# Comparing the second half of each edge list with three destinations, in a graph network kernel

## What is computed

```python
edge_index = jnp.stack([src, dst])
agg = jax.ops.segment_sum(edge_attr, dst, num_segments=N)      # edge features, per destination
h_sum = jax.ops.segment_sum(h[src], dst, num_segments=N)       # in several layers
deg = jax.ops.segment_sum(ones, dst, num_segments=N)
```

## Time and profile before

| what | us |
|---|---|
| median of 3 executions | 850.17 |
| lowest and highest | 847.88 and 850.56 |
| span of the profiled execution | 857.5 |
| of it the counting stage, up to the end of the last L1629 | 256.8 |

### The profile page before, as it was taken

How to read it: one execution, slowest core, us unless ns; L and a number is a source line. 1 busy time by engine, 2 the same in 40 slices (tenths; PEclk the granted TensorE clock), 3 DMA queues, 4 the chain that set the end, 5 groups by cost and what they waited for, 6 DMA issues and landing times.

```text
span 857.5 us, 16017 instructions
## 1 busy us (share of the span) xinstructions
PE 789.4 (92%) x6335; PEld 713.4 (83%) x6335; DVE 610.7 (71%) x973; ACT 325.1 (38%) x580; POOL 21.8 (3%) x39
## 2 busy tenths in 40 slices
PE   5699999998997999989998999969987999999995
PEld 2589999998997999889998998535546999699994
DVE  6998999998886676777876874657567455035654
ACT  0234545454356322332245332345335332432233
POOL 3500000000000000000000000000000000000000
PEclk9558999999797999999998999989999999999998
DMA  5446787877662100000000000000000000000001
GB/s 106 100 102 139 159 188 164 190 167 166 146 132 54 39 1 1 1 2 1 1 1 21 1 1 3 0 1 13 1 0 26 0 0 1 1 1 1 1 25 52
DMA packets 161334, 43.00 MB, mean 50 GB/s; under 512 B 155080, under 2 KB 159761, under 8 KB 161189
## 3 DMA queue, kind: packets, MB, share of 16 engines
q1 hardware_dynamic: 148042, 39.81, 20.8%
q10 hardware_dynamic: 11932, 0.81, 1.0%
q0 software_dynamic: 1280, 1.29, 0.6%
HBM read 39.07 MB, written 2.01 MB: 48 GB/s over the span
## 4 chain that ended last, share of the span: by engine, by line
PE 76%; DVE 12%; SPq 4%; issue 3%; DMA 2%; ACT 2%; POOL 0%; DVEq 0%; ACTq 0%
PE bank L1694 20%; PE bank L1695 20%; PE bank L1629 11%; PE bank L1619 7%; PE bank L1902 2%; SPq L551 2%; PE bank L1910 1%; PE bank L1756 1%; PE bank L1953 1%; PE bank L1954 1%; PE bank L1707 1%; SPq L553 1%; PE bank L1769 1%; DVE wb L1236 1%; DVE counts L968 1%
## 5 line engine op out<-in xcount | busy, mean ns | idle before, releaser
L1694 PE MATMUL bank<-stage,f_hi 125*128 125x392 f32 x1000 | 347.8, 348 | 3.5 <-issue 2.2
L1695 PE MATMUL bank<-stage,f_lo 125*128 125x392 f32 x1000 | 341.6, 342 | 0.0
L1114 DVE CAST stage<-counts 125x2352 fp32r<-125x2352 uint8 x120 | 164.3, 1380 | 80.9 <-PE bank L1695 80.7
L776 ACT ACTIVATE stage<-counts 125x1568 fp32r<-125x1568 uint8 x80 | 108.1, 1351 | 226.8 <-PE bank L1695 224.5
L1694 PEld LDWEIGHTS bank<-stage,f_hi 125*128 125x128 f32 x1000 | 189.2, 189 | 5.1 <-issue 4.0
L1695 PEld LDWEIGHTS bank<-stage,f_lo 125*128 125x128 f32 x1000 | 189.1, 189 | 0.6
L1629 PE MATMUL bank<-tmp,wb 128*65 128x25 f32 x2000 | 139.3, 225 | 1.7 <-DVE tmp L1072 1.7
L1629 PEld LDWEIGHTS bank<-tmp,wb 128*65 128x65 f32 x2000 | 136.0, 150 | 2.6 <-DVE tmp L1072 2.4
L729 ACT ACTIVATE counts<-bank 125x500 uint8<-125x500 f32 x188 | 88.6, 537 | 47.3 <-PE bank L1619 45.6
L1619 PE MATMUL bank<-rowb,xT 128*128 128x125 bf16 x1250 | 92.5, 233 | 9.7 <-DVE rowb L1050 5.3
L1047 DVE TENSOR_TENSOR xT<-xT,tmp 128x2560 bf16<-128x2560 bf16 (+1 forms) x63 | 92.8, 1473 | 5.1 <-PE bank L1619 5.0
(11 more groups left out here) (223 smaller groups left out, 670.5 us busy)
## 6 DMA issues: line engine op xcount, KB each, us to landing
wb<-in_edge_attr SPq DMA_DIRECT2D x125, 256.0 KB, 3.9
wa<-in_x SPq DMA_DIRECT2D x12, 125.0 KB
out<-wl SPq DMA_DIRECT2D x6, 250.0 KB
xT<-in_dst SPq DMA_DIRECT2D x63, 4.0 KB, 3.5
xT<-in_dst ACTq DMA_DIRECT2D x62, 4.0 KB, 3.1
eaT<-eaT SPq DMA_DIRECT2D x1, 784.0 KB, 6.3
wb<-in_L_gnn_w_ih SPq DMA_DIRECT2D x1, 384.0 KB, 3.4
gate_w_d<-wl SPq DMA_DIRECT2D x1, 384.0 KB, 3.0
```

The lines of the kernel that those rows point to most:

```text
L776: nc.scalar.activation(set_buffer(u, m), counts[:, SETS[u][0]:sum(SETS[u]), chunk(c)], ACT.Copy).then_inc(s["set_a_ready"], 1)
L1114: nc.vector.tensor_copy(set_buffer(u, m), counts[:, SETS[u][0]:sum(SETS[u]), chunk(pair * 2 + off)]).then_inc(s["set_d_ready"], 1)
L1694: mm(bank[h][:, 0:CH], f_hi[:, first + k, :], rhs[:, k, :], start=(first + k == 0), stop=False)
L1695: last = mm(bank[h][:, 0:CH], f_lo[:, first + k, :], rhs[:, k, :], start=False, stop=(first + k == HI - 1))
```

## The change

Blocks are still 5 destinations with two lists of 128 edges. But the second list is now compared with the destinations 2, 3 and 4 of its block only. So the second matmul of a block has 75 moving columns (L1670 of the new kernel; the first, L1666, keeps 125).

To make these one-hot rows in one VectorE instruction per group, the kept key list becomes eight copies for every two blocks, `PARTS_KEY`: the first list with five shifts (keys minus 0, 25, 50, 75, 100) and the second with three (minus 50, 75, 100). Each copy is compared with 0 to 24. The key comparison writes 128x2000 instead of 128x2500. The two neighbouring elements of the inner dimension are now two blocks, where they were the two lists of a block. The copies are written by ScalarE when lists are kept: eight or sixteen small activations with a constant added instead of one. They lie in three tiles (rowb, wl1, wl3).

The low-digit comparison writes 125 columns per list instead of 128 (128x2500 instead of 128x2560); the columns 125 to 127 are set to zero once by GpSimd, and the weights keep 128 columns.

Lists are now kept 126 blocks at a time, at the blocks 0, 126, 252, 378 and 500, so that a pair of blocks isn't cut. For the last group, whose last block's list is moved back to end at the last edge, the destinations 0 and 1 of the second list are compared too (`oh_last`, one more matmul of 50 columns per block, five in all). A block whose edge in slot 128 still belongs to destination 0 or 1 sets the flag to the general path: two more small VectorE instructions in group 5. GpSimd makes six short iotas where there were two, three memsets and one select more.

```diff
 UNITS = [(g, i, n) for g in range(NGP) for i, n in ((0, 4), (4, 3), (7, 3)) if g * GB + i + n <= NBK] + [(NGP - 1, 4, 1)]
 NU = len(UNITS)
 UB = 5
-QL = 125
-NQ = NBK // QL
+QL = 126
+NQ = 5
+Q_AT = (0, QL, 2 * QL, 3 * QL, NBK + 1 - QL)
 SLOTS = 256
+PARTS_KEY = ((0, 0), (0, 1), (0, 2), (0, 3), (0, 4), (1, 2), (1, 3), (1, 4))
+NK = len(PARTS_KEY)
+KEPT_AT = (0, 270, 540, NBK + 1)
 EW = 25
 NE = N // EW
 TE = 8
...
-        nl, nk = GB * 128 * 2, GB * BK * 2
+        nl, nk = GB * 128 * 2, GB * NK * HI
         oh_lo = [xT_bf[:, r * nl:(r + 1) * nl].rearrange("p (b l j) -> p b l j", l=128, j=2) for r in range(2)]
-        oh_key = [rowb_bf[:, r * nk:(r + 1) * nk].rearrange("p (b k j) -> p b k j", k=BK, j=2) for r in range(2)]
-        key_list = rowb_bf[:, 2 * nk:2 * nk + 2 * NBK].rearrange("p (b j) -> p b j", j=2)
+        oh_key = [rowb_bf[:, r * nk:(r + 1) * nk].rearrange("p (b m k j) -> p b m k j", m=NK, k=HI, j=2) for r in range(2)]
+        nk_list = (KEPT_AT[1] - KEPT_AT[0]) * NK
+        key_list = [a[:, 0:(KEPT_AT[i + 1] - KEPT_AT[i]) * NK].rearrange("p (b m j) -> p b m j", m=NK, j=2)
+                    for i, a in enumerate((rowb_bf[:, 2 * nk:], wl1[:, 400:400 + nk_list // 2].bitcast(BF16), wl3[:, 256:600].bitcast(BF16)))]
+        last_at = NGP * GB - GB
+        key_last = wl3[:, 600:606].bitcast(BF16).rearrange("p (b m j) -> p b m j", m=2, j=2)
         nh = 2 * TE * EW
         oh_dst = [tmp_f[:, r * nh:(r + 1) * nh].rearrange("p (j w) -> p j w", w=EW) for r in range(2)]
-        lo_list = tmp_f[:, 2 * nh:2 * nh + NBK].bitcast(BF16).rearrange("p (b j) -> p b j", j=2)
+        lo_list = tmp_f[:, 2 * nh:2 * nh + NBK + 1].bitcast(BF16).rearrange("p (b j) -> p b j", j=2)
         at = [nl]
 
         def carve(n):
...
         past_block = carve(NQ)
+        past_two = carve(NQ)
+        oh_last = carve(3 * 2 * HI).bitcast(BF16).rearrange("p (b m k j) -> p b m k j", m=2, k=HI, j=2)
         crowded = carve(NQ)
         list_idx = carve(NQ).bitcast(I32)
...
                            allow_small_or_imprecise_dtypes=True)
-            nc.gpsimd.iota(key_base, pattern=[[-QL * BK, NQ]], base=0, channel_multiplier=-BK,
-                           allow_small_or_imprecise_dtypes=True)
-            nc.gpsimd.iota(past_block, pattern=[[QL * BW, NQ]], base=BW, channel_multiplier=BW,
-                           allow_small_or_imprecise_dtypes=True)
+            for a, n in ((0, NQ - 1), (NQ - 1, 1)):
+                nc.gpsimd.iota(key_base[:, a:a + n], pattern=[[-QL * BK, n]], base=-Q_AT[a] * BK, channel_multiplier=-BK,
+                               allow_small_or_imprecise_dtypes=True)
+                nc.gpsimd.iota(past_block[:, a:a + n], pattern=[[QL * BW, n]], base=Q_AT[a] * BW + BW, channel_multiplier=BW,
+                               allow_small_or_imprecise_dtypes=True)
+                nc.gpsimd.iota(past_two[:, a:a + n], pattern=[[QL * BW, n]], base=Q_AT[a] * BW + 2, channel_multiplier=BW,
+                               allow_small_or_imprecise_dtypes=True).then_inc(s["pool_w"], 1)
+            for r in range(2):
+                nc.gpsimd.memset(oh_lo[r][:, :, LO:D, :], 0.0)
+            pool.wait_ge(s["pool_w"], 5)
+            nc.gpsimd.affine_select(out=past_two[:, NQ - 1:NQ], in_=past_two[:, NQ - 1:NQ], compare_op=ALU.is_gt, fill=-1.0, base=last_at - Q_AT[NQ - 1],
+                                    pattern=[[0, 1]], channel_multiplier=-1)
             for r in range(RE):
                 last = nc.gpsimd.memset(ea_in[r][:, :, DE:DE + 1], 1.0)
             last.then_inc(s["slots_clean"], 1)
...
             def keep_lists(q):
 
-                for k, kept in enumerate((lo_list, key_list)):
-                    act.wait_ge(s["list_t"], 2 * q + 2)
-                    nc.scalar.activation(kept[:, q * QL:(q + 1) * QL, :],
-                                         bank[7][:, :].bitcast(BF16)[:, k * 256:(k + 1) * 256].rearrange("p (j c) -> p c j", j=2)[:, 0:QL, :],
-                                         ACT.Copy).then_inc(s["list_kept"], 1)
+                a, b = Q_AT[q], Q_AT[q] + QL
+                turned = [bank[7][:, :].bitcast(BF16)[:, k * 256:(k + 1) * 256].rearrange("p (j c) -> p j c", j=2) for k in range(2)]
+                act.wait_ge(s["list_t"], 2 * q + 2)
+                nc.scalar.activation(lo_list[:, a:b, :], turned[0].rearrange("p j c -> p c j")[:, 0:QL, :], ACT.Copy).then_inc(s["list_kept"], 1)
+                for i, kept in enumerate(key_list):
+                    c, d = max(a, KEPT_AT[i]), min(b, KEPT_AT[i + 1])
+                    if c < d:
+                        for m, (j, w) in enumerate(PARTS_KEY):
+                            last = nc.scalar.activation(kept[:, (c - KEPT_AT[i]) // 2:(d - KEPT_AT[i]) // 2, m, :],
+                                                        turned[1][:, j, c - a:d - a].rearrange("p (b j) -> p b j", j=2), ACT.Copy, bias=-float(HI * w))
+                if q == NQ - 1:
+                    for m in range(2):
+                        last = nc.scalar.activation(key_last[:, :, m, :], turned[1][:, 1, last_at - a:QL].rearrange("p (b j) -> p b j", j=2),
+                                                    ACT.Copy, bias=-float(HI * m))
+                last.then_inc(s["list_kept"], 1)
 
             def odd_list(e):
 
...
-                dve.wait_ge(s["list_kept"], 2 * ((b0 + n - 1) // QL) + 2)
+                dve.wait_ge(s["list_kept"], 2 * min((b0 + n - 1) // QL, NQ - 1) + 2)
                 if g >= 2:
                     dve.wait_ge(s["unit_made"], units_until(g - 2))
-                nc.vector.tensor_tensor(oh_lo[r][:, 0:n, :, :], iota_l.rearrange("p (a l) j -> p a l j", a=1).to_broadcast([128, n, 128, 2]),
-                                        lo_list[:, b0:b0 + n, :].rearrange("p b (a j) -> p b a j", a=1).to_broadcast([128, n, 128, 2]),
+                nc.vector.tensor_tensor(oh_lo[r][:, 0:n, 0:LO, :], iota_l.rearrange("p (a l) j -> p a l j", a=1)[:, :, 0:LO, :].to_broadcast([128, n, LO, 2]),
+                                        lo_list[:, b0:b0 + n, :].rearrange("p b (a j) -> p b a j", a=1).to_broadcast([128, n, LO, 2]),
                                         ALU.is_equal).then_inc(s["lo_hot"], 1)
-                nc.vector.tensor_tensor(oh_key[r][:, 0:n, :, :], iota_l.rearrange("p (a l) j -> p a l j", a=1)[:, :, 0:BK, :].to_broadcast([128, n, BK, 2]),
-                                        key_list[:, b0:b0 + n, :].rearrange("p b (a j) -> p b a j", a=1).to_broadcast([128, n, BK, 2]),
-                                        ALU.is_equal).then_inc(s["key_hot"], 1)
+                half = -(-n // 2)
+                i = sum(b0 >= a for a in KEPT_AT[1:3])
+                here = (b0 - KEPT_AT[i]) // 2
+                hot = nc.vector.tensor_tensor(oh_key[r][:, 0:half, :, :, :].rearrange("p b m k j -> p (b m) k j"),
+                                              iota_l.rearrange("p (a l) j -> p a l j", a=1)[:, :, 0:HI, :].to_broadcast([128, half * NK, HI, 2]),
+                                              key_list[i][:, here:here + half, :, :].rearrange("p b m (a j) -> p (b m) a j", a=1).to_broadcast([128, half * NK, HI, 2]),
+                                              ALU.is_equal)
+                if g == NGP - 1:
+                    hot = nc.vector.tensor_tensor(oh_last.rearrange("p b m k j -> p (b m) k j"),
+                                                  iota_l.rearrange("p (a l) j -> p a l j", a=1)[:, :, 0:HI, :].to_broadcast([128, 6, HI, 2]),
+                                                  key_last.rearrange("p b m (a j) -> p (b m) a j", a=1).to_broadcast([128, 6, HI, 2]),
+                                                  ALU.is_equal)
+                hot.then_inc(s["key_hot"], 1)
                 if 1 <= g + 1 < NQ:
                     make_lists(g + 1)
                 if g == NQ:
...
+                    nc.vector.tensor_tensor(past_two[:QL, :], lists_i.rearrange("p (q s) -> p q s", q=NQ)[:, :, D], past_two[:QL, :],
+                                            ALU.is_lt).then_inc(s["dve_w"], 1)
                     dve.wait_ge(s["dve_w"], landed.next())
-                    nc.vector.tensor_tensor(g_bad[:LO, :], g_bad[:LO, :], g_most[:LO, :], ALU.max).then_inc(s["flag_part"], 1)
+                    nc.vector.tensor_tensor(crowded[:QL, :], crowded[:QL, :], past_two[:QL, :], ALU.max).then_inc(s["dve_w"], 1)
+                    dve.wait_ge(s["dve_w"], landed.next())
+                    nc.vector.tensor_reduce(g_most[:QL, :], crowded[:QL, :], AX.X, ALU.max).then_inc(s["dve_w"], 1)
+                    dve.wait_ge(s["dve_w"], landed.next())
+                    nc.vector.tensor_tensor(g_bad[:QL, :], g_bad[:QL, :], g_most[:QL, :], ALU.max).then_inc(s["flag_part"], 1)
 
                 es = edge_blocks(g)
                 ne = len(es)
...
-                        for j in range(2):
```

(24 more changed lines are left out.)

32 lines of the change are left out of this document (16 added, 16 removed).

## The result

The changed kernel takes 957.16 us (median of four executions, 956.37 to 957.82), against 850.37 us for the kernel before (four executions, 847.88 to 851.75). The ratio is 1.126, with a 95% interval from 1.123 to 1.130. The forecast was 948 us, from 878 to 978.

A forecast was written before the change was run, and what follows sets the result against it. TensorE was taken to bound the kernel at 1.2 GHz (5.56 us a group), with TensorE, VectorE and SyncE close at 2.4. A stage ending 98.3 us later, added to the 850.2 us median, gave 948 us, range 878 to 978.

The forecast's parts named there:

- The clock: Counting stage: the thinner product run no longer suffices to raise TensorE's clock, which stays at 1.2 GHz from about 50 us.
- The faster rival: Counting stage: the clock rises all the same and loads set the pace; 845 us, between 838 and 850; 17%.
- A group at 1.2 GHz: Ten blocks on TensorE in the counting stage: edge sums 3.46 us plus product run 1.68, together 5.14 us.
- The start: Groups 0 to 3: shorter comparisons save 1.2 us, copies cost 0.3; edge sums of group 3 start at 50.8 us.
- The second matmul: TensorE's product matmuls: 75 columns take 63 ns at 1.2 GHz; about 60 ns either way at 2.4, gaining nothing.
- The other bound: Product matmul of 75 columns at 1.2 GHz: 105 ns if something besides moving columns sets it; group stays 5.56 us.
- VectorE: Counting stage comparisons: 540 to 560 fewer elements save 0.3 us, giving 2.97 us a group; key comparison near 1.16 us.
- ScalarE's copies: Keeping lists as small shifted copies: first eight delay the first comparison by nothing to 1.4 us, taken as 0.3.
- The joint behind the stage: Transposes after the counting stage: up to 2.9 us more at 1.2 GHz, hidden behind destination degrees, taken as 0.
- The stage and the span: Counting stage ends at 355.1 us, 98.3 us later; later layers untouched; profiled span 955.8 us.
- the last step: From span to median: the median's distance of 7.3 us below the profiled span is kept, giving 948.5 us.
- SyncE's 3.37 us a group: Issuing a group's loads in the counting stage: 3.37 us, untouched by the change, setting the pace at 2.4 GHz.

The follow-up runs named there:

- b_second_75: Kernel before, second matmul of a block cut to 75 columns in every group, counts wrong; stage ended at 358.4 us, whole execution 23839.9 us with the general path.
- e_before_75_right: Kernel before, second matmul at 75 columns in all groups but the last, which keeps 125, so outputs are right; 961.16 us, ratio 1.130 to the kernel before.
- f_before_100: Kernel before, second matmul at 100 columns in all groups but the last; 970.11 us, ratio 1.141 to the kernel before.
- c_after_edge_50: Changed kernel, each edge-sum matmul moving its 25 columns twice (50); 846.04 us, ratio 0.9944 to the kernel before.
- h_after_edge_50_act: Changed kernel with 50-column edge sums and all destination-number loads issued by ScalarE; 829.82 us, ratio 0.9756 to the kernel before.
- before: The kernel without the change; 850.37 us, median of four executions.
- after: The changed kernel as it was measured, without further edits; 957.16 us, median of four executions.

## Why the prediction was right, and where it was off

The forecast's mechanism is the one that was found, and its range held the time. That the span came out within 1.1 us owes something to luck, since errors of about 2 us cancelled. By its own steps:

- **The clock.** Predicted: once lost about 50 us, it stays at 1.2 GHz to the end of the stage. Measured: 0.50 from 24.1 us on. The kernel before was at 0.50 from 25 us too; what didn't take place is the short rise near 45 us. That cost nothing that can be seen: the edge sums of group 3 start earlier than before all the same. The reason given, that the run of twenty product matmuls sufficed only just, is borne out by the runs: the shorter matmul alone takes the clock away (b_second_75, e_before_75_right), 100 columns don't keep it (f_before_100), and moved columns put back in another line bring it back (c_after_edge_50). It wasn't predicted that edge sums could do as well as the product run. The prediction had said of L1629 only that it never did with its 25 columns.
- **The faster rival**, that a TensorE without pauses comes up all the same, had 17%. The 306.5 us without a pause in e_before_75_right are against it, and c_after_edge_50, less busy and at 2.4 GHz, is too. Part 1 of the Trainium skill's page "TensorE: Matmul & The Clock Gate", which has the clock follow how busy TensorE was, doesn't hold in this trace as it stands: at the same number of matmuls with the same weights, the moving columns made the difference.
- **A group at 1.2 GHz.** Predicted 5.14 us, measured 5.18. The product run is 1.69 us instead of 1.68, L1680 3.49 instead of 3.46. Over 59 groups that is 2.4 us.
- **The start.** The edge sums of group 3, from which the sum counts, were put at 50.8 us, and they start at 48.7. The forecast counted the shorter comparisons (1.2 us) and 0.3 us for the copies. It missed that the kernel before had lost 1.19 us in group 0 waiting for gathered sources, a wait that is gone in this execution, and that the first comparison begins 0.4 us sooner. Why the wait is gone is open. These 2.1 us hide the 2.4 us of the line above.
- **The second matmul.** 63 ns were taken, with 105 as the other bound. A pair now takes 169 ns (1.69 us for ten pairs); with 105 ns for the first, that leaves 64. The other bound is out. At 2.4 GHz the prediction was wrong: it said "about 60 ns either way", so that nothing is gained there. The product run takes 0.96 us instead of 1.18 (h_after_edge_50_act), which is 37 ns for a matmul of 75 columns beside 59 for one of 125. So TensorE, put at 3.04 us a group in the faster rival, isn't what would hold the changed kernel at the full clock; VectorE is, with 2.97. The forecast of 948 us didn't depend on it. The rule of the Trainium skill on LDWEIGHTS ("TensorE: Matmul & The Clock Gate"), 107 ns for 128 weight columns, isn't seen here; its section on weight-path perf modes, by which 128 weights that aren't float32 load faster, agrees.
- **VectorE.** 2.97 us a group predicted, 2.97 measured in c_after_edge_50. L1085 was said to come near 1.16 us; it takes 1.19, and 1.11 to 1.14 us lie between its start and the next one's in c_after_edge_50.
- **ScalarE's copies.** Taken at 0.3 us on the path, measured at 0: the first eight take 1.46 us, some 0.16 us apart, and end at 25.1 us, before the first comparison at 25.6.
- **The joint behind the stage.** L1642's doubling was put at 0, hidden behind the degrees. It is hidden but for its end: the transposes are on the chain of waits, and the flag behind them comes a few tenths of a us later than the degrees would allow.
- **The stage and the span.** Predicted end 355.1 us, measured 355.7. Predicted span 955.8 us, measured 954.7: what follows the stage took 599.0 us, against 600.7 in the profiled execution of before. In the other runs that don't take the general path it is 599.4 to 601.2 us, so most of this is no effect of the change.

**The term that was mis-sized** is the last step, the distance between span and median. "The median of the runs lies 7.3 us below that span, and I keep this distance": that gave 948.5 us instead of 957. The distance was no constant. In after, the profiled execution's time is its span plus 1.7 us, so the profiled execution of before had taken about 859 us, far up among its executions (38 over all comparisons, from 845.19 to 855.86, and one of 860.09). It was one that lost the clock for 13.6 us from 212.8 on the earlier trace rows. If the rest takes some 600 us in every execution, a median one has a stage of about 249 us (an estimate: 850.4 less 1.7 and 600), 8 us less than the profiled 256.8. How the clock went in the others isn't known, as no trace of them was kept, but their mean granted clock falls in the main with the time, from 0.964 at 845.19 us to 0.949 at 855.86, and it was 0.946 in the profiled one. In the changed kernel, where the clock is never up in the stage, there is nothing of the kind to lose: its four executions lie within 1.5 us. The right step was to add the 1.7 us to the new span of 955.8, 957.5 us. Of the two ways to read the change, 97.2 us between spans and 106.8 us between medians, the second is the difference of typical executions.

What the forecast said of the loads, that SyncE's 3.37 us a group would set the pace as soon as VectorE needs less, was priced only in the rival. c_after_edge_50 shows its waits, and h_after_edge_50_act takes them away and gains 16.2 us. What stays open is what decides a short rise in the list groups: b_second_75 had one (39.2 to 42.6 us), and e_before_75_right had none, though the two issue the same instructions up to the last group. So the program alone doesn't decide it, and one profile each doesn't tell more.

## What to carry to other kernels

Before making the matmuls of a tight stage smaller, look at the granted clock of that stage, and at what TensorE moved right before it rose: 40% fewer columns in one of two product matmuls would have saved TensorE 0.2 us a group at 2.4 GHz, where it isn't the bound, and cost 107 us by leaving the engine at 1.2. A thin matmul with few moving columns can be made thicker for next to nothing, as the edge sums were, and this decides for the change or against it (957 or 846 us). And when a shorter comparison should bring a gain, ask which queue is next: here the small loads had to leave SyncE's queue before the 17.5 us could be had.

## What was not expected of the hardware

- TensorE without a pause over 306.5 us and 3073 matmuls stays at 1.2 GHz. With 50 instead of 25 moving columns in the edge sums it holds 2.4 GHz over 194 us with 15 us of pauses. At 2.4 GHz these wider matmuls cost next to nothing: a run of 32 takes 1.90 us in h_after_edge_50_act, and 1.86 us with 25 columns in the kernel before.
- Fewer columns can be faster or slower, depending on the clock. At 1.2 GHz 100 columns give 970 us, 75 give 961, and 125, which bring the clock back, 850.
- At 2.4 GHz a matmul of 75 columns behind 128 bf16 weight columns has 37 ns, one of 125 has 59, and one of 25 behind 65 float32 weight columns 58 (1.86 us for 32).
- The kernel at the margin of the clock seems to vary more: before ranges over 3.9 us in its first four executions and over 10.7 us in 19, after over 1.5 us in four and c_after_edge_50 over 5.2 us in ten. With so few executions this is no more than a sign.
